# An attention and FFN layer: weight sums in six places and stored from GpSimd's queue, and the residual path of the FFN stage in another order

## The reference

```
n   = layernorm(x)
a   = softmax(q k^T / 4) v      16 heads of 16; q, k, v from n by weights alpha * sign(W), plus a bias
x1  = x + layernorm(a Wp + bp)  Wp also alpha * sign(W)
n1  = layernorm(x1)
h   = silu(n1 W1 * s1) * (n1 W2 * s2)          256 -> 1024, ternary weights, a scale per column
h   = gelu(h H1 * sh1);  h = gelu(h H2 * sh2)  1024 x 1024 each
out = x1 + layernorm(h W3 * s3)                1024 -> 256
```

## Time and profile before

| | us |
|---|---|
| runs | 1197.98, 1195.18, 1197.16 |
| median | 1197.16 |
| the profiled execution | 1199.53 |
| its span | 1197.8 |
| PE, ACT, DVE, GpSimd busy in it | 1145.4, 918.6, 755.8, 88.6 |

### The profile page before, as it was taken

One profiled execution on the slowest core, in us unless ns is written; L12 is line 12 of the kernel. 1 busy time (PEld: TensorE's weight loads), 2 busy tenths in 40 slices (PEclk: granted clock), 3 DMA queues, 4 the chain that ended last, 5 costly groups with the idle time before them and its releaser, 6 DMA issues.

```text
span 1197.8 us, 21087 instructions
## 1 busy us (share of the span) xinstructions
PE 1145.4 (96%) x8241; PEld 778.0 (65%) x8241; DVE 755.8 (63%) x1165; ACT 918.6 (77%) x1218; POOL 88.6 (7%) x140
## 2 busy tenths in 40 slices
PE   6699999999999999898999999999999999999997
PEld 4233323332333322225999999989989999899897
DVE  7354525353436246895767767768678677686766
ACT  6689999999999999795675676757756766577565
POOL 6001000101010000000010000010100000101000
PEclk9799999999999999899999999999999999999999
DMA  5989768976899589834330431423404314233031
GB/s 180 238 213 230 190 103 194 225 182 103 198 212 202 103 187 199 221 123 152 100 138 30 142 125 61 151 92 110 141 35 141 125 55 145 101 110 138 4 124 55
DMA packets 67031, 166.96 MB, mean 139 GB/s; under 512 B 10102, under 2 KB 27126, under 8 KB 60774
## 3 DMA queue, kind: packets, MB, share of 16 engines
q1 hardware_dynamic: 66636, 165.12, 51.2%
q10 hardware_dynamic: 288, 0.39, 0.1%
HBM read 122.18 MB, written 52.40 MB: 146 GB/s over the span
## 4 chain that ended last, share of the span: by engine, by line
PE 32%; DVE 10%; ACT 6%; issue 3%; POOL 2%; DVEq 0%; ACTq 0%
PE ffn_ps L1876 21%; DVE op_lo L2130 4%; PE ffn_ps L1814 4%; PE ffn_ps L1815 4%; ACT op_hi L1991 3%; PE ffn_ps L1889 3%; ACT feed L2020 2%; PE side_ps L1781 1%; DVE feed L2123 1%; ACT zn L2026 1%; DVE ln_stats L2108 1%; DVE feed L2148 1%; ACT L2020 1%; POOL ln_shift L1701 1%; DVE feed L2141 1%
## 5 line engine op out<-in xcount | busy, mean ns | idle before, releaser
L1286 ACT ACTIVATE probs<-s_ps 128x1024 f32<-128x1024 f32 x512 | 475.5, 1115 | 36.0 <-PE s_ps L1131 35.4
L1145 PE MATMUL y_ps<-probs,v_st 128*17 128x512 f32 x2048 | 272.7, 605 | 9.1 <-DVE y_sb L1311 8.1
L1876 PE MATMUL ffn_ps<-op_hi,W 128*128 128x256 f32 x1024 | 240.5, 279 | 0.0
L1876 PE MATMUL ffn_ps<-op_lo,W 128*128 128x256 f32 x1024 | 240.5, 279 | 0.0
L2130 DVE TENSOR_TENSOR op_lo<-feed,op_hi 128x1024 fp32r<-128x1024 f32 x144 | 174.7, 1222 | 95.3 <-ACT op_hi L1991 95.3
L1131 PEld LDWEIGHTS s_ps<-q_st,k_st 50*128 50x128 f32 x1024 | 88.4, 187 | 209.9 <-ACT probs L1286 172.0
L1131 PE MATMUL s_ps<-q_st,k_st 50*128 50x512 f32 x1024 | 207.4, 470 | 7.8 <-DVE y_ps L1521 7.3
L1876 PEld LDWEIGHTS ffn_ps<-op_hi,W 128*128 128x128 f32 x1024 | 193.3, 189 | 0.3
L1876 PEld LDWEIGHTS ffn_ps<-op_lo,W 128*128 128x128 f32 x1024 | 191.7, 187 | 0.3
L1876 PE MATMUL ffn_ps<-op_hi,sums_of_w 128*128 128x256 f32 x768 | 186.8, 284 | 0.5 <-ACT feed L2007 0.5
L1876 PE MATMUL ffn_ps<-op_lo,sums_of_w 128*128 128x256 f32 x768 | 186.0, 283 | 0.0
(11 more groups left out here) (199 smaller groups left out, 1308.8 us busy)
## 6 DMA issues: line engine op xcount, KB each, us to landing
sums_of_w<-sum_scr SPq DMA_DIRECT2D x48, 1024.0 KB, 5.0
k_st<-qk_scr SPq DMA_DIRECT2D x90, 128.0 KB, 6.5
q_st<-qk_scr SPq DMA_DIRECT2D x90, 128.0 KB, 7.0
w_scr<-ffn_w SPq DMA_DIRECT2D x16, 704.0 KB, 8.0
W<-w_scr SPq DMA_DIRECT2D x16, 704.0 KB, 5.9
y_scr<-y_sb SPq DMA_DIRECT2D x32, 256.0 KB, 4.0
qk_scr<-y SPq DMA_DIRECT2D x24, 256.0 KB, 6.8
qk_scr<-sums SPq DMA_DIRECT2D x24, 256.0 KB, 7.9
```

The lines of the kernel that those rows point to most:

```text
L1145: i = pe.matmul(y_ps[32 * j:32 * j + VCOLS, :], v_st[g % 2][:, s, VCOLS * j:VCOLS * (j + 1)], probs[(PAIRS * turn + j // 2) % PROBS][:, j ...
L1286: act.activation(probs[a % PROBS][:, :, :], s_ps[a % 3][:, :, :], ACT.Exp, scale=SCALE)\
L1876: mm = pe.matmul(dst[:, a * HB:(a + 1) * HB], w, part[slot][:, kt // 2, cols].bitcast(form), start=(fresh and kt == 0 and a == 0 and part ...
```

## The change

Attention, batch 3. Sums 0 to 15 go through six places instead of four, the two new ones in the buffer `xb`, which is `zn`; sums 16 to 31 go through four as before. The stores are counted by three semaphores instead of two, and DVE waits for those of the pairs that held its places. GpSimd issues the stores instead of SyncE, at the same turns. The softmax sums of the first tail block are loaded as 64 per partition, inverted by one reciprocal at turn 22, written to HBM and read back spread over the rows at turn 24.

Tail. PE projects y behind product 2 of layer 0 instead of 3, and turns x1 behind product 5 of layer 1 instead of between the output tiles. ACT normalises Z behind `high(10)` instead of `high(13)`, X1 behind `high(13)` instead of `high(15)`, and takes the high part of x1 between the two gelus of Q12 instead of at the end. DVE's steps of this path move with them; `low(3)` and `low_of_y` come ahead of `add_c11(0, 0)`, and `low_of_x1` ahead of `add_c12(1, 1)`.

```diff
+def load_few_sums(sp, y_scr, few_sums, b, u, done):
+    y_blk = y_scr.rearrange("(b c a d) t -> b c a d t", b=BATCH, c=CT, d=2 * HEAD_DIM)
+    for c in range(CT):
+        few = y_blk[b, c, :, HEAD_DIM, u * BLK:(u + 1) * BLK].rearrange("a (s f) -> a s f", s=HEAD_DIM // 2)
+        sp.dma_start(few_sums[c * HALF:(c + 1) * HALF, :], few).then_inc(done, 16)
+def store_inverses(sp, inv_scr, few_sums, done):
+    sp.dma_start(inv_scr.rearrange("h (s f) -> (h s) f", s=HEAD_DIM // 2), few_sums).then_inc(done, 16)
+def spread_inverses(sp, inv_scr, tail_in):
+    for c in range(CT):
+        heads = HEADS // CT
+        sp.dma_start(tail_in.sums[:, c, :], inv_scr[c * heads:(c + 1) * heads, :].unsqueeze(1)
+                     .to_broadcast([heads, HEAD_DIM, BLK])).then_inc(tail_in.y_loaded, 16)
...
         def sum_at(j):
-            if j % 4 < 2:
-                return qk[j % 4][:, :]
-            return v_aug[...][:, (j % 4 - 2) * HM:(j % 4 - 1) * HM]
+            n = j % 6 if j < SUM_UNITS // 2 else j % 4
+            if n < 2:
+                return qk[n][:, :]
+            if n < 4:
+                return v_aug[...][:, (n - 2) * HM:(n - 1) * HM]
+            return xb[:, :, :].rearrange("p t c -> p (t c)")[:, (n - 4) * HM:(n - 3) * HM]
+        def wait_sum_stores(eng, pairs):
+            for r in range(3):
+                n = len(range(r, pairs, 3))
+                if n:
+                    eng.wait_ge(sum_stored[r], 32 * n)
...
(SyncE, prepared)
-                if t in SUM_TURNS:
-                    store_sum(SUM_TURNS.index(t))
                 if t == 11:
...
+                    load_few_sums(sp, y_scr, few_sums, 0, 0, few_loaded)
                     load_tail_y(sp, y_scr, tail_in, 0, 0)
+                if t == 24:
+                    sp.wait_ge(tail_in.inverted, 1)
+                    store_inverses(sp, inv_scr, few_sums, inv_stored)
+                    sp.wait_ge(inv_stored, 16)
+                    spread_inverses(sp, inv_scr, tail_in)
(GpSimd)
+            def store_sum(j):
...
+                pool.wait_ge(sum_made, j + 1)
+                pool.dma_start(dst, sum_at(j)).then_inc(sum_stored[j // 2 % 3], 16)
...
-            ln_rstd(PROJECTED)
-            ln_rstd(PROJECTED + 1)
+            for t in range(TURNS_OF_BATCH):
+                if t in SUM_TURNS:
+                    store_sum(SUM_TURNS.index(t))
+                if t == 40:
+                    ln_rstd(PROJECTED)
+                if t == 46:
+                    ln_rstd(PROJECTED + 1)
(VectorE, attention)
-                if j >= 4:
-                    dve.wait_ge(sum_stored[j // 2 % 2], 32 * (j // 4))
+                wait_sum_stores(dve, j // 2 - (2 if j < SUM_UNITS // 2 else 1))
...
-                if t in (24, 26, 28, 30):
-                    invert_sums(dve, tail_in, 0, (t - 24) // 2)
+                if t == 22:
+                    dve.wait_ge(few_loaded, 16 * CT)
+                    dve.reciprocal(few_sums, few_sums).then_inc(tail_in.inverted, 1)
...
+                if t == 36:
+                    wait_sum_stores(dve, 6)
(TensorE, tail)
-                    if ahead and k == K_U2:
+                    if ahead and k == K_Z:
                         project_y(i)
                 for k in range(NP):
                     product(i, 1, k)
+                    if ahead and k == K_C21:
+                        turn_x1(i)
                 if ahead:
                     out_tiles(i, 0)
-                    turn_x1(i)
                     out_tiles(i, 1)
(ScalarE, tail)
                 high(i, 10)
+                if ahead:
+                    normalise(Z, i + 1, zn, zn, z_norm)
...
                 high(i, 13)
                 if ahead:
-                    normalise(Z, i + 1, zn, zn, z_norm)
+                    normalise(X1, i + 1, zn, x1[1 - u], x1_norm)
...
                 high(i, 15)
+                gelu(i, 1, Q12, 0)
                 if ahead:
-                    normalise(X1, i + 1, zn, x1[1 - u], x1_norm)
-                gelu(i, 1, Q12, 0)
+                    high_of_x1(i)
                 gelu(i, 1, Q12, 1)
                 high(i, 16)
                 high(i, 17)
-                if ahead:
-                    high_of_x1(i)
(VectorE, tail)
                 make_t(i, 0, 3)
+                low(i, 3)
+                if ahead:
+                    low_of_y(i)
                 add_c11(i, 0, 0)
-                low(i, 3)
                 add_c11(i, 0, 1)
                 make_t(i, 0, 4)
                 low(i, 4)
                 if ahead:
-                    low_of_y(i)
+                    scale_z(i)
...
                 low(i, 11)
+                if ahead:
+                    add_x(i, 1 - u, ahead[0])
                 low(i, 12)
+                if ahead:
+                    dve.wait_ge(x1_done, i + 1)
+                    stats_of(X1, x1[1 - u], range(TILES))
+                    mean_var_of(X1, i + 1)
                 low(i, 13)
                 add_c22(i, 1, 0)
                 add_c22(i, 1, 1)
-                if ahead:
-                    add_x(i, 1 - u, ahead[0])
-                    dve.wait_ge(x1_done, i + 1)
-                    stats_of(X1, x1[1 - u], range(TILES))
...
                 low(i, 15)
+                if ahead:
+                    low_of_x1(i)
                 add_c12(i, 1, 1)
                 low(i, 16)
                 low(i, 17)
                 if ahead:
-                    low_of_x1(i)
                     scale_out(i)
```

More of the change, by code:

```diff
@@ L300, in layer @@
         )
-        attention(nc, c, qk_scr, v_scr, m_scr, y_scr, ffn_w, w_scr, sum_scr, W, quads, first, x, tail_in, spent)
+        attention(nc, c, qk_scr, v_scr, m_scr, y_scr, ffn_w, w_scr, sum_scr, W, quads, first, x, tail_in, inv_scr, spent)
         until_ffn.close()
@@ L746, in project, with attention @@
     return range(x_loaded[0].num, lo_first_stored.num + 1)
-def attention(nc, const, qk_scr, v_scr, m_scr, y_scr, ffn_w, w_scr, sum_scr, W, quads, first, x, tail_in, spent):
+def attention(nc, const, qk_scr, v_scr, m_scr, y_scr, ffn_w, w_scr, sum_scr, W, quads, first, x, tail_in, inv_scr, spent):
     m_rows = m_scr.rearrange("s h (i p) -> (h i) s p", p=P)
@@ L795, in attention @@
         group_top = sb("pj_group_top", [P, GROUPS], F32)
+        few_sums = group_top[:, 0:FEW]
         square = sb("pj_square", [P, QK, GROUPS], BF16)
@@ L858, in attention @@
         sum_checked = sem("sum_checked")
-        sum_stored = [sem(f"sum_stored{i}") for i in range(2)]
+        sum_stored = [sem(f"sum_stored{i}") for i in range(3)]
+        few_loaded = sem("at_few_loaded")
+        inv_stored = sem("at_inv_stored")
         Y_HI, Y_LO, Z_SCALED, Z_BIASED, Z_ADDED = 1, 2, 3, 5, 6
@@ L1054, in _ @@
             store_y(HALVES - 1)
-            for pair in range(2):
-                sp.wait_ge(sum_stored[pair], 16 * SUM_UNITS // 2)
+            wait_sum_stores(sp, SUM_UNITS // 2)
         @block.gpsimd
@@ L1073, in root @@
                 pool.tensor_tensor(bound[:, :], product[:, :], half[:, :], ALU.pow).then_inc(root_done, 1)
+            def store_sum(j):
+                l, kt, kind = j // 16, j % 16 // 4, SUM_KINDS[j % 4]
+                if kind == "S1":
+                    dst = quarter_of_w(l, kt, 1, 0)
+                else:
+                    dst = sum_scr[len(STREAMED) * l + STREAMED.index(kind), :, kt * HM:(kt + 1) * HM]
+                pool.wait_ge(sum_made, j + 1)
+                pool.dma_start(dst, sum_at(j)).then_inc(sum_stored[j // 2 % 3], 16)
             pool.sem_clear(spent)
@@ L1727, in load_y, with load_inverses @@
             def load_y(i, b, u):
-                y_blk = y_scr.rearrange("(b c a d) t -> b c a d t", b=BATCH, c=CT, d=2 * HEAD_DIM)
-                tokens = slice(u * BLK, (u + 1) * BLK)
                 if not is_zero(i):
                     sp.wait_ge(y_lo_done, i)
[L1733 to L1739, removed]
+                load_few_sums(sp, y_scr, few_sums[:, :], b, u, few_loaded)
+                load_tail_y(sp, y_scr, tail_in, b, u)
+            def load_inverses(i):
                 sp.wait_ge(few_inverted, i + 1)
-                sp.dma_start(inv_scr.rearrange("h (s f) -> (h s) f", s=HEAD_DIM // 2), few_sums[:, :]).then_inc(inv_stored, 16)
+                store_inverses(sp, inv_scr, few_sums[:, :], inv_stored)
                 sp.wait_ge(inv_stored, 16 * (i + 1))
[L1743 to L1746, removed]
+                spread_inverses(sp, inv_scr, tail_in)
             def store(f):
@@ L1756, in step @@
                     load_y(i, *ahead)
-                    spread_inverses(i)
+                    load_inverses(i)
                 stream(i, 2)
@@ L2296, in step @@
                 low(i, 8)
-                add_c12(i, 0, 1)
                 if ahead:
                     mean_var_of(Z, i + 1)
+                add_c12(i, 0, 1)
                 make_t(i, 1, 1)
@@ L2312, in step @@
                 add_c22(i, 1, 1)
-                if ahead:
-                    add_x(i, 1 - u, ahead[0])
```

(6 more changed lines are left out.)

35 lines of the change are left out of this document (7 added, 28 removed).

## The result

The changed kernel takes 1225.62 us (median of 4 runs, 1225.22 to 1229.44) against 1196.75 for the kernel before in the same comparison: ratio 1.0249, 95% interval 1.0225 to 1.0273. It is slower by 2.5%. The forecast was 1220, with a range of 1209 to 1230. The profiled execution took 1225.82 us, span 1224.0, so it lies at its own median, which the profiled execution of the kernel before did not (2.4 above it).

What follows compares the result with a forecast made beforehand. PE, busy 96% of the span, was taken as the bound, its tail waits paid in full. Terms -6 + 1 + 10.5 + 13.3 + 4.5 = +23.3 on 1199.53 gave 1222.8, less 2.4: 1220 us, range 1209 to 1230.

Steps and rivals of the forecast that it cites:

- Attention, -6: Last attention batch: ACT's idle time goes because the copy of y is no longer late; about 6 us saved, bounds 0 and 8.
- +1 for the late stores: Attention turns 54 to 61: stores from GpSimd's queue land later and DVE waits to reuse places; 1 us lost, about 6 at most.
- both causes: Last attention batch: DVE's 4.98 us wait for a store and four wide reciprocals, 7.0 us together, make the copy of y late.
- Rival (d): Attention: stores from GpSimd land so late that DVE still waits and the 6 us aren't won; 1226, chance 8%.
- Its 5 us more: Stores from GpSimd: by the skill's rule DVE starves them, landing nears the upper end, the sum up to 5 us more, 1225.
- First layer, 10.5: Tail, first layer: gelu, copy_u2 and product 4 come 1.7 us later in six blocks, block 7 about 0.3; 10.5 us lost.
- Second layer, 13.3: Tail, second layer: ACT stands 3.9 us for X1's input, low(16) comes late; 1.9 us in seven blocks, 13.3 lost.
- Clock, 4.5: Tail, longer idle stretch of PE before operand 16: clock drops costing 1.5 us in three of seven blocks; 4.5, bounds 0 and 10.5.
- The 2.4 taken off: Whole kernel: the profiled execution, 1199.53 us, was 2.4 above the median 1197.16, so 2.4 came off the sum.
- Rival (a): Tail, second layer: X1's chain is in time for ACT and the 1.5 stall goes in seven blocks; 1192, faster, chance 7%.
- rival (b): Tail: only the first layer is late; gaps on ACT and DVE absorb the second layer's 3.9 us; 1203, chance 10%.
- Rival (c): Tail: the clock falls in all seven blocks, or for 6 us; 1226 to 1229, chance 13%.

Runs made afterwards that it cites:

- e1: Changed kernel's attention stage with the tail of the kernel before: 1192.02 us, ratio 0.9949 to the kernel before.
- e12: As e8, but of attention's changes only the small reciprocal; four places for weight sums, stores from SyncE: 1184.28 us, ratio 0.9891.
- e11: Kernel before with only the 32 stores of weight sums issued from GpSimd instead of SyncE: 1192.43 us, ratio 0.9954.
- e6: As e1, but with four places for weight sums as before; stores from GpSimd and one small reciprocal stay: 1192.00 us, ratio 0.9948.
- e5: As e1, but stores of weight sums issued from SyncE as before; six places and the small reciprocal stay: 1193.60 us, ratio 0.9966.
- e4: Changed kernel with the tail's second layer put back to its old order: 1205.17 us, ratio 1.0049 to the kernel before.
- e3: Changed kernel with the tail's first layer put back to its old order: 1204.45 us, ratio 1.0052 to the kernel before.
- e9: Changed kernel with 16 more matmuls of constants filling PE's idle stretch before operand 16: 1220.88 us, ratio 1.0206 to the kernel before.
- e10: Changed kernel with the first half's add_c11 back in front of low(3) and low part of y on DVE: 1215.96 us, ratio 1.0158.
- e2: Attention of the kernel before with the changed kernel's tail: 1228.48 us, ratio 1.0266 to the kernel before.
- e8: Changed attention, old tail with Z's normalisation, add_x and X1's statistics moved earlier, X1's normalisation, turns and split as before: 1182.09 us, ratio 0.9869.
- e7: As e1, but with the four wide reciprocals as before and six places for weight sums: 1193.32 us, ratio 0.9961.

## Why the prediction was right, and where its terms were off

The sign, the range and the mechanism held; its own forecast of the likeliest case (1213 to 1228) too. By its steps, on the profiled execution (1222.8 predicted, 1225.8 measured):

- **Attention, -6 and +1 for the late stores:** 6.6 in the profile, 6.1 in e1. The number is right, the working was not. It failed where it said that the stores "matter only in turns 54 to 61": the one that DVE waited for belongs to turn 19, and it was issued 6.5 us after its sum was ready. (The wait itself stands in turn 25, not in turn 18 as I read it.) And "both causes" didn't have to go: the small reciprocal alone (e12) or the queue alone (e11) is enough; six places alone weren't tried. The wait itself goes with the store's earlier issue (e6, e11) as well as with six places (e5); I had seen only the second way. The prediction had read when DVE waited and for which store, but not when that store was issued. Rival (d) was priced from the wrong side: the queue didn't endanger the gain, in e11 it carries it whole. The +1 isn't seen: PE's wait for row_bits stayed at 0.3. Its row, 5.0 us to landing, was a median over the whole batch; the stores that the kernel before issued from 527 us on landed in 2.2 to 2.4. SyncE's added steps weren't "nothing" on DVE: in the changed kernel the division waits 2.83 us for the inverses (to 478.78). Room covered it, since the copy of y at 482.12 waits 2.12 more for PE; that is about 5 us of room where 12 was said.
- The Trainium skill's rule (SBUF — State Buffer, SBUF: two separate sides), by which DVE's fast-mode operations starve DMAs issued from GpSimd, isn't borne out at this size: stores landed 5.4 us after issue at the median in the changed kernel (2.3 to 13.6), 4.4 in the kernel before (2.2 to 12.4), 8.3 in e5 from SyncE and 5.1 in e11 from GpSimd. Its 5 us more did not come. Whether DVE's operations beside these stores were in that fast mode, no row shows.
- **First layer, 10.5:** right. 11.3 less 0.5 is 10.8; e4's periods give 10.7. Gelu late by 1.7, product 4 by 1.76, block 7 by 0.3 (0.80 for 0.52).
- **Second layer, 13.3:** 12.5 by e3's periods. ACT stood 3.87 for X1 (3.9 predicted). The sum went by when operand 16 is ready, so the 0.6 at add_c22, kept only as a bound, did come in all seven blocks without adding up: PE reaches the next wait later by as much and waits so much less there (a wait of 2.41 where 2.8 to 3.4 was foreseen).
- **Clock, 4.5:** the mis-sized term, 9.0. The size of one drop was right (1.5), their number was six and not three. It is also what set the runs apart from one another: e3 and e4 have one drop each, e9 moved the drops to another stretch, e10 halved them.
- **The 2.4 taken off:** it was the distance of one execution from its median, a fair guess beforehand, and that the changed kernel's own execution lay at its median is chance. The kernel before's was slow in attention: e2, with the same attention, began its tail at 548.88, 2.6 sooner. The seven profiles with the whole of the changed attention begin it between 542.4 and 545.1, so the 6.6 of two single profiles is good to 2 us or so. The 2.4 and the 4.5 that the clock's term lacked make 6.9 of under-estimate, against 2.4 of over-estimate in attention and the second layer; the difference is most of the 5.6 by which 1220 fell short. The terms as measured (-6.1, 10.7, 12.5 and 9.0) make 26.1, and the two profiled executions differ by 26.3; the medians differ by 28.9. The 2.8 that are left aren't tied to a step.

Rival (a) needed the X1 chain in time, which it missed by 3.87; rival (b) needed gaps to take that in, and 12.5 came through. Rival (c), all seven blocks, was nearly the case, with six.

What stays open is what decides whether the clock falls. It fell behind idle stretches of 2.0 to 2.7 in some blocks and not in others (counts below): it held behind 2.04 in the changed kernel and fell behind the same 2.04 in e9. No run shows the cause; that it hangs on where in time the stretch falls, which the equal periods of 85.3 in a row would fit, is an argument, not shown.

## What to carry to other kernels

When an engine waits for a store, read the time of the store's issue as well as its landing: a store in a queue that also loads waits for every load in front of it (6.5 us behind 15 loads here), and another queue can be enough, without more buffers (e11). In a strictly ordered queue move the makers of a late operand forward, not the step that consumes it: the consumer, moved to where its input isn't ready, makes everything behind it wait (3.87 us here); e8, which moved Z's normalisation and DVE's steps ahead of X1's and left X1's normalisation in its place, gained. When PE bounds the kernel and gets new idle stretches of the size seen here, 2.0 to 2.7 us, put a drop of its clock (1.5 us here) behind each of them as the upper bound.

## What the runs showed that I had not expected

- A drop of the clock isn't fixed by the length of the idle stretch before it. Behind 2.67 of idle PE it fell in 6 of 7 blocks in the changed kernel and e2, 3 of 7 in e10, 1 of 7 in e3; behind 2.04 in none of 6 in the changed kernel and e2, 1 of 6 in e4, 5 of 6 in e9; behind 1.75 (from the last transpose to the second output tile), in the kernel before and in e1, e4 to e7 and e11, in none of 49. In no block did it fall behind both stretches.
- At the change of stage the same wait of 2.8 us was followed by anything from no low clock (e9: PEclk 1.00 from 543) to some 6 us at 1.2 GHz (e1: 0.50 from 543 to 548). In e1 block 0 took 82.99, in e6, with the same tail and no low clock there, 80.16. That is up to 3 us between executions of one tail.
- One DMA of 256 KB, issued behind 15 loads of a quad, took 10.1 us to land; the median over all 32 such stores was 4.4. Issued by GpSimd in the middle of the same loads (e11) it took 8.2.
- The issue of such a store takes 0.54 us on GpSimd (e11, median) and 0.32 to 0.59 on SyncE (kernel before).
